# Cross-attention in tile pairs: context projections one tile less ahead of the scores, no extra projection where the pairs begin, and GpSimd takes a tile's keys before the next context

## The reference

```
x = x + cross_attention(layernorm(x), context)   # context: 6272 x 256, 32 heads of 8, RMS norm of q and k
x = x + self_attention(layernorm(x))             # 64 tokens, 16 heads of 128, weights = codes * scales
x = x + experts(layernorm(x))                    # 8 experts (top 2) and a shared one
```

## Time and profile before

| what | value |
|---|---|
| median of the runs | 207.59 us |
| profiled execution: device time, span | 208.22 us, 206.4 us |
| TensorE matmul busy | 193.7 us (94%) |
| ScalarE busy | 148.6 us (72%) |
| VectorE busy | 124.7 us (60%) |
| GpSimd busy | 109.5 us (53%) |
| granted TensorE clock | full in all 40 slices |
| DMA engines, mean busy share | 90% or more in nearly every slice of the cross-attention |

### The profile page before, as it was taken

How to read it: one execution, slowest core, us unless ns; L and a number is a source line. 1 busy time by engine, 2 the same in 40 slices (tenths; PEclk the granted TensorE clock), 3 DMA queues, 4 the chain that set the end, 5 groups by cost and what they waited for, 6 DMA issues and landing times.

```text
span 206.4 us, 7072 instructions
## 1 busy us (share of the span) xinstructions
PE 193.7 (94%) x2625; PEld 133.0 (64%) x2625; DVE 124.7 (60%) x326; ACT 148.6 (72%) x286; POOL 109.5 (53%) x131
## 2 busy tenths in 40 slices
PE   7796987999999999999999999999997989999995
PEld 3364564777777777777777777777764553559554
DVE  1588868566767766677676667767533052463680
ACT  2474885889888888998888889888869912342240
POOL 6445759488666848857684885768475001000100
PEclk9999999999999999999999999999999999999999
DMA  6679999999999999999899899999985599100000
GB/s 195 174 195 205 169 234 213 211 175 245 248 208 237 215 223 233 173 259 210 216 210 240 215 210 254 207 259 203 254 198 110 174 405 430 64 0 3 3 0 13
DMA packets 66549, 39.70 MB, mean 192 GB/s; under 512 B 53858, under 2 KB 60642, under 8 KB 66402
## 3 DMA queue, kind: packets, MB, share of 16 engines
q1 hardware_dynamic: 66098, 38.98, 85.8%
q10 hardware_dynamic: 432, 0.46, 0.7%
HBM read 26.52 MB, written 0.07 MB: 129 GB/s over the span
## 4 chain that ended last, share of the span: by engine, by line
PE 71%; ACT 7%; issue 6%; DMA 5%; DVE 5%; POOL 3%; SPq 1%; DVEq 0%; ACTq 0%; POOLq 0%
PE ps L885 17%; PE ps L907 10%; PE ps L862 10%; PE ps L910 8%; PE ps L913 8%; PE ps L960 5%; ACT room L464 4%; DMA kT<-k 3%; PE ps L1054 3%; DMA wkv_f<-xwkv 2%; PE ps L1013 2%; PE ps L1072 2%; PE ps L819 1%; POOL w_all L385 1%; PE ps L999 1%
## 5 line engine op out<-in xcount | busy, mean ns | idle before, releaser
L464 ACT ACTIVATE room<-ps 128x1024 f32<-128x1024 f32 x98 | 95.3, 1023 | 1.8 <-PE ps L862 1.6
L403 POOL TENSOR_TENSOR ctx_lo<-ctx_f,ctx_hi 128x256 fp32r<-128x256 f32 x49 | 36.0, 734 | 43.6 <-DVE ctx_hi L640 40.6
L885 PE MATMUL ps<-room,v_sb 128*27 128x192 f32 (+1 forms) x1176 | 48.4, 310 | 0.2 <-ACT room L464 0.2
L907 PE MATMUL ps<-wkv_hi,ctx_hi 128*128 128x512 f32 x98 | 41.9, 428 | 2.4 <-DVE k L671 2.1
L910 PE MATMUL ps<-wkv_lo,ctx_hi 128*128 128x512 f32 x98 | 39.0, 398 | 1.2 <-DVE wkv_lo L592 1.2
L885 PEld LDWEIGHTS ps<-room,v_sb 128*27 128x27 f32 (+1 forms) x1176 | 32.8, 103 | 11.0 <-ACT room L464 0.6
L385 POOL TENSOR_TENSOR w_all<-w_all,s_ring 128x1024 f32<-128x1024 f32 x16 | 38.2, 2390 | 0.0
L647 DVE TENSOR_REDUCE k_ss<-k_sq 128x32 f32<-128x256 f32 x49 | 20.3, 415 | 29.2 <-ACT k_sq L471 29.2
L390 POOL TENSOR_TENSOR k<-k_n,k 128x256 f16<-128x256 f32 x49 | 32.9, 673 | 6.7 <-DVE k L671 6.7
L862 PE MATMUL ps<-q_blk,kT 48*128 48x128 f16 x784 | 31.5, 218 | 3.9 <-ACT room L464 2.1
L862 PEld LDWEIGHTS ps<-q_blk,kT 48*128 48x128 f16 x784 | 22.0, 94 | 19.1 <-issue 11.0
(11 more groups left out here) (117 smaller groups left out, 134.2 us busy)
## 6 DMA issues: line engine op xcount, KB each, us to landing
w_all<-codes SPq DMA_DIRECT2D x16, 512.0 KB, 4.2
ctx_f<-ctx_t SPq DMA_DIRECT2D x48, 128.0 KB, 3.6
up_sb<-up_w SPq DMA_DIRECT2D x5, 704.0 KB, 7.4
s_ring<-scales SPq DMA_DIRECT2D x12, 256.0 KB
s_ring<-wo_scales SPq DMA_DIRECT2D x4, 512.0 KB
dn_sb<-down_w SPq DMA_DIRECT2D x1, 1792.0 KB, 14.0
kT<-k SPq DMA_TRANSPOSE x49, 4.3
wkv_f<-xwkv SPq DMA_DIRECT2D x1, 256.0 KB, 3.9
```

The costliest lines, as they stand in the source:

```text
L403: nc.gpsimd.tensor_tensor(ctx_lo[:, split.slot(2)], ctx_f[:, split.slot(4)], ctx_hi[:, split.slot(2)].bitcast(F32), ALU.subtract).then_inc ...
L464: nc.scalar.activation(probs[:, t.probs_slot(), half], ps_scores[half].rearrange("p b n -> p (b n)"), ACT.Exp).then_inc(exp_done, 1)
L885: last = nc.tensor.matmul(ps_o[bank][CT * j:CT * j + heads * VW, at:at + heads * N], v_sb[:, t.slot(8), slot:slot + heads].rearrange("p h ...
L907: nc.tensor.matmul(dst, ctx_hi[:, a, c], wkv_hi[:, c], start=(c == 0), stop=False)
```

## The change

The distances become PROJ = 5, KV = 4, TR = 3, and the pairs now run from step 5 to step 44 = T-5. An odd step t of the pairs is scores(t), projections of t+4 and t+5; the even step is as before. So the first tile that is projected in a pair is now odd, where it was even. In the steps by themselves at the beginning, step 3 now makes scores(3), values(2) and projection 8, step 4 scores(4) and values(3) and no projection, and step 5 starts the pairs with projections 9 and 10. At the end step 43 makes projections 47 and 48 one behind the other (before, step 43 was by itself, with values(42) and projection 48), and step 44 makes values(42) and values(43). ScalarE's special case for step 3 goes. On GpSimd the second part of the keys of tile t+3 now always stands ahead of `ctx_lo` of tile t+6; the multiplications of the weights stay behind the same pair of tiles. The two runs of zero matmuls behind the cross-attention become 5 and 2 instead of 7 and 4. VectorE's and SyncE's lists name the same tiles in the same order as before. The hardware loop now begins at step 6 and has 4 rounds as before.

```diff
-PROJ, KV, TR, PV = 5, 5, 4, -1
-FIRST, LAST = -(PROJ + 2), T - PV
-HEAD = 4
-LOOP0 = 4
-PAIR0, PAIR1 = 3, T - PROJ - 2
-ITERS = (T - PROJ - 2 - LOOP0) // U
+PROJ, KV, TR, PV = 5, 4, 3, -1
+FIRST, LAST = -(PROJ + 1), T - PV
+HEAD = KV
+PAIR0, PAIR1 = 5, T - PROJ
+LOOP0 = PAIR0 + 1
+ITERS = (T - PROJ - 1 - LOOP0) // U
...
     (GpSimd)
-                split, keys = t.ahead(PROJ + 2), t.ahead(TR)
-                if keys.exists() and c < -1:
+                split, keys = t.ahead(PROJ + 1), t.ahead(TR)
+                if keys.exists():
                     second_part(keys)
                 if split.exists():
...
-                if keys.exists() and c >= -1:
-                    second_part(keys)
-                u, piece = divmod(c + 1 - DEQ0, DEQ)
+                u, piece = divmod(c - DEQ0, DEQ)
...
     (ScalarE)
-                if t.i is None and t.c == PAIR0:
-                    exps(t, 0)
-                    keys_squared(r.ahead(-1))
-                    exps(t, 1)
-                    keys_rms(r.ahead(-1))
-                else:
-                    exps(t, 0)
-                    exps(t, 1)
+                exps(t, 0)
+                exps(t, 1)
...
     (TensorE)
-                    if kv.exists() and t.c != -1:
+                    if kv.exists() and t.c not in (-1, PAIR0 - 1):
                         project_context(kv)
                 elif t.odd():
+                    project_context(kv.ahead(-1))
                     project_context(kv)
-                    project_context(kv.ahead(1))
                 else:
-                    for k in (pv.ahead(-1), pv):
-                        for group in range(len(GROUPS)):
-                            values(k, group)
+                    all_values(pv.ahead(-1))
+                    all_values(pv)
...
-            keep_busy(7)
+            keep_busy(5)
...
-            keep_busy(4)
+            keep_busy(2)
```

More of the change, by code:

```diff
@@ L97, in probs_slot, with singly @@
         return 0 if self.odd() else 1 + self.c // 2 % 2
+    def singly(self):
+        return self.i is None and not PAIR0 <= self.c <= PAIR1
     def count(self, per=1, plus=0):
@@ L490, in step @@
                 r = t.ahead(KV)
-                if singly(t):
-                    r = t.ahead(KV - 1 if t.c < PAIR0 else KV)
+                if t.singly():
                     if t.exists():
@@ L628, in split_context @@
             def split_context(t):
-                split = t.ahead(PROJ + 2)
+                split = t.ahead(PROJ + 1)
                 if split.i is None and split.c < 2:
@@ L691, in step @@
                     keys_scaled(r)
-            steps(dve, step, {-5: queries_squared, -4: queries_placed})
+            steps(dve, step, {-4: queries_squared, -3: queries_placed})
             dve.wait_ge(ready("o_first"), 1)
@@ L914, in project_context, with all_values @@
                 last.then_inc(kv_mm, 1)
+            def all_values(pv):
+                for group in range(len(GROUPS)):
+                    if pv.exists():
+                        values(pv, group)
             def step(t):
-                kv, pv = t.ahead(PROJ), t.ahead(PV)
+                pv, kv = t.ahead(PV), t.ahead(PROJ)
                 for half in range(2):
@@ L920, in step @@
                         scores(t, half)
-                if singly(t):
-                    for group in range(len(GROUPS)):
-                        if pv.exists():
-                            values(pv, group)
+                if t.singly():
+                    all_values(pv)
                     if t.c == 0:
                         project_context(kv.ahead(-1))
-                    if kv.exists() and t.c != -1:
+                    if kv.exists() and t.c not in (-1, PAIR0 - 1):
                         project_context(kv)
                 elif t.odd():
+                    project_context(kv.ahead(-1))
                     project_context(kv)
-                    project_context(kv.ahead(1))
                 else:
-                    for k in (pv.ahead(-1), pv):
-                        for group in range(len(GROUPS)):
-                            values(k, group)
+                    all_values(pv.ahead(-1))
+                    all_values(pv)
             steps(pe, step, {-5: queries_mm, -2: queries_turned})
```

2 lines of the change are left out of this document (removed).

## The result

The changed kernel takes 206.62 us, the median of five executions (205.55 to 210.05), beside 207.79 for the kernel before in the same comparison: a ratio of 0.9924, with an interval of 0.9898 to 0.9951. That is 1.2 to 1.6 us faster, where 3.0 were forecast (204.6), and the time lies 0.12 above the range of 203.5 to 206.5. Two later comparisons gave 206.35 (0.9923, 0.988 to 0.9965) and 207.03 (0.9939, 0.9907 to 0.9972).

What follows compares the result with a forecast made beforehand. TensorE was taken as the bound of the pairs, with ScalarE almost a second. Profiled 208.22 less 2.5 (cross-attention) and 0.45 (zero matmuls) gave 205.3, less 0.63 to the median 204.6 us; range 203.5 to 206.5.

Steps and rivals of the forecast that it cites:

- What bounds the kernel: Pairs of tiles: TensorE is the bound with a beat of 5.98 us, ScalarE almost a second bound.
- Opening: Steps 3 to 7: projections 8 and 9 stop waiting, tile 7's exponentials at 40.9 instead of 43.38, 2.5 us earlier.
- The first rival: Opening half won: new waits or late keys 5 leave a gain of 1.2 instead of 2.5; 206.3 us, chance 0.20.
- GpSimd's order: Keys ahead of ctx_lo on GpSimd: turnings issue sooner; ctx_lo 0.67 later within a cover of 1.0, so costs nothing.
- the reorder does nothing: Rival: turning waits behind a load anyway, six first tiles miss by 0.8; 208.7's size, within that rival's chance of 0.09.
- Keys' slack: Keys' time before their scores falls to 9.7 and 11.9 us; waits at tiles 40, 41, 43, 0.8 in sum.
- End: From tile 43's exponentials to the last values: ScalarE's 1.79 wait gone, 14.3 us against 14.7.
- Zero matmuls: Behind the cross-attention and ahead of the third norm: shorter runs of zeros save 0.25 and 0.2, together 0.45 us.
- The rule on the clock: Fewer zeros in a wait could drop TensorE's clock to half behind them; as a rival 208 us, chance 0.02.
- Keys as the bound of the middle: Rival: with transfers of 5.4, six first tiles behind a multiplication wait 0.75 each; 208.7 us, chance 0.09.
- no keys late at all: Fourth rival: no scores wait for keys, so the 0.8 us drops out; 203.8 us, chance 0.14.
- Sum: Whole kernel: profiled execution 208.22 less 2.5 and 0.45 is 205.3; median 0.63 below that, 204.6 us.

Runs made afterwards that it cites:

- e1: Changed kernel with only the shift of the pairs: GpSimd's old order and zero matmuls of 7 and 4 kept; 215.36 us, ratio 1.0365.
- e3: Kernel before with only the zero matmuls changed, 5 and 2 instead of 7 and 4; 207.36 us, ratio 0.9984.
- e7: Kernel before with only the end changed: steps 43 and 44 a pair, tile 48's logarithm and exponential between tile 44's halves; 205.86 us, ratio 0.9912.
- e2: Kernel before with only GpSimd's order changed, the keys' second part always ahead of ctx_lo; 207.49 us, ratio 0.9996.
- a2: The changed kernel measured a second time, nothing altered; 206.35 us over nine executions, ratio 0.9923.
- a10: The changed kernel measured a third time, nothing altered; 207.03 us over 12 executions, ratio 0.9939.
- e6: Kernel before with its old key lead kept, pairs from step 5, another end, GpSimd's new order, zeros 5 and 2; 204.75 us, ratio 0.987.
- e8: Changed kernel with tile 48's logarithm and exponential between the halves of tile 44's exponentials; 205.74 us, ratio 0.9909.
- e9: Changed kernel with SyncE's loads of scales issued one tile later; 206.33 us, ratio 0.9919.
- e11: The same kernel as e6, measured once more beside the changed kernel; 204.54 us, ratio 0.9825.
- e4_light: Changed kernel loading only 16 columns of each piece of codes and scales, multiplications on a cleared buffer (two memsets); 205.08 us, ratio 0.9878.
- e5_light: Changed kernel loading only 16 columns of each piece, without the two memsets, multiplications reading other resident data; 204.59 us, ratio 0.9838.

## Why the prediction was wrong

The mechanisms came as forecast: both gaps closed, and keys became late. The step that failed is the term for late keys, 0.8 us in the sum. The profiles show 1.5, 2.75 and 2.5 in its place (1.8 by the medians), and 1.15 and 1.25 of it in the two typical executions lie in the end, which the sum had at nothing: above all the landing of tile 48, which had been priced at 0.6 and then left out. The second step that failed is the subtraction of 0.63 from a profiled execution to the median.

- **What bounds the kernel: right.** Steady beats of 5.98 us (107.55 / 18 = 5.975 with no key late).
- **Opening: right.** Forecast 12.26 from scores(3) to tile 7's exponentials, 12.12 without late keys, 12.17 to 12.51 with them. "So its wait is gone" held for both projections. The first rival named tile 5's keys, and they did come late, but it put the opening's gain at 1.2, and it is 2.2 to 2.6 (14.74 less 12.12 to 12.51). That its sum, 206.3, lies near the measured time is luck.
- **GpSimd's order: right for its other side** (no wait of TensorE for `ctx_lo` in the pairs), **and undervalued.** The rival "the reorder does nothing" put its absence at 208.7; without it the kernel took 213.0 to 217.5. Six tiles times 0.8 was the wrong form of sum, since tiles of the opening and of the end were late as well: these make 6.6 of the 8.84 us of waits.
- **Keys' slack: the step that failed.** "I take 0.8 for the sum" stood beside tiles 40, 41 and 43. The three profiles give C less 107.55: 1.07, 1.25 and 1.16. To that come 0.39, 0.35 and 0.05 in the opening and 0.06, 1.15 and 1.25 in D. Tiles 40 and 41 were expected and were late in every profile of the changed kernel. Two things in the working were off.

  First, "5.0 at most before 118 us" was the longest of one execution of one kernel. Four profiles with GpSimd's old order (before, e1, e3, e7) have 5.0 to 5.9 there; eight with its new order and the full loads (e2, after, a2, a10, e6, e8, e9, e11) have 6.2 to 7.3, and between 28 and 60 us a median of 4.8 to 5.3 against 4.3 to 4.8. So the longer transfers go with the earlier turnings of the new order, though barely where the opening is the old one (e2: 6.2 and 4.8); what makes them longer is not shown.

  Second, "the turning is issued 0.05 behind" leaves out SyncE's own time. In the kernel before this was there already: tile 8's turning begins 1.48 after its second part. In order of time on the changed kernel's queue around tile 5 (turning 4, context 11, scales, turning 5), then around tile 14 (turning 13, context 20, scales, turning 14):

```profile
25.28 1.23 SPq L309 DMA_TRANSPOSE kT<-k  x1
26.61 0.72 SPq L301 DMA_DIRECT2D ctx_f<-ctx_t  x1
27.39 0.66 SPq L318 DMA_DIRECT2D s_ring<-scales  x1
28.14 1.84 SPq L309 DMA_TRANSPOSE kT<-k  x1
```
```profile
54.10 1.24 SPq L309 DMA_TRANSPOSE kT<-k  x1
55.45 0.51 SPq L301 DMA_DIRECT2D ctx_f<-ctx_t  x1
56.02 0.66 SPq L318 DMA_DIRECT2D s_ring<-scales  x1
56.77 1.26 SPq L309 DMA_TRANSPOSE kT<-k  x1
```

  Tile 14's second part ended at 55.41; its turning begins at 56.77, 1.36 later, because issuing takes the queue 2.67 us from one turning to the next there. Tiles 5 and 8 lose 1.42 and 1.31 in the same place of the order, and both come late in all three profiles (transfers of 6.0 to 6.8 on top). The prediction watched the first tiles of pairs (13, 19, 25, 31), which were never late in the changed kernel.
- **End: the mechanism right (14.31), the typical size not.** "What is late next is this landing: at 4.1 instead of 3.1 it costs 0.6" was priced and left out of the sum. It was 4.45 and 4.55 in the two typical executions, tile 46 was late before it, and D 15.46 and 15.56: 1.2 to 1.3 over the forecast. This is the largest missing term of these two.
- **Zero matmuls: right**, 0.45. The rule on the clock that was weighed against it did nothing here: the granted clock is 1.00 in the stretch behind the shortened run (166.00 to 168.00) and in every later slice:

```profile
166.00:168.00 2.00, 1.61 (x10) 0.94 (x10) 1.67 (x10) 0.20 (x1) 0.00 (x0) 1.00 1.07 418
```

- **The other rivals.** Keys as the bound of the middle (208.7) did not come about with GpSimd's new order; no keys late at all (203.8) is what e4_light and e5_light had to be built for.
- **Sum: the subtraction failed.** "The median of the runs was 0.63 below the profiled one" was carried over from one kernel to the other. For the changed kernel the median lies 1.07 above its profiled execution. The forecast for that execution, 205.3, missed by 0.25; with 0.63 and 1.07 this is 1.95 of the 2.0 missed. That the 0.25 is so small is the luck of a fast execution; the two typical ones (206.35 and 206.90) miss by 1.1 and 1.6. Put the other way, by e5_light: late keys cost 1.8 instead of 0.8, and 204.59 without any stands 0.8 above the 203.8 of the fourth rival, about the 0.63 that did not carry over.

Before, the keys had 13.3 and 14.3 us and only tiles 40 and 41 were near their limit, so the time hardly depended on the transfers. With 9.7 and 11.9 the set of late tiles differs from execution to execution (tile 11 in two of the three profiles, 17 and 23 in one, 48 in two). That this also makes the spread of the times is argued and not shown: part A moves by up to 2.7 us as well.

What stays open: why GpSimd's new order goes with longer transfers in the opening, and why even the kernel without weight traffic has executions in two groups (203.5 to 204.1 and 205.1 to 205.6); of these only one was profiled.

## What to carry to other kernels

Slack before a DMA is insurance: when an edit spends it, take the wait from the longest transfer of several executions plus the issuing queue's own time per DMA, for every position in the period, and put it into the sum. One profile is one draw; when the slack is gone, do not carry a median minus a profiled time from the old kernel to the new one (-0.63 became +1.07 here). An edit that is worth nothing by itself (the order on one engine) can be what makes another possible, so it must be tested with it. And a kernel that wins the ends without spending the lead in the middle was here the better one.

## What the runs showed of the hardware

Two VectorE instructions took as long as the GpSimd memsets beside them. In e4_light, VectorE's and then GpSimd's order of time near the start:

```profile
3.61 1.98 DVE L552 TENSOR_SCALAR spread<-twins,row_sum 128x128 f32<-128x128 f32 x1 [0.68 <-POOL twins L368]
3.81 1.78 DVE L555 BATCH_NORM_STATS2 bn<-x_sb 128x6 f32<-128x128 f32 x1
```
```profile
3.44 0.28 POOL L371 CAST ident<-ident 128x128 f16<-128x128 f32 x1
3.68 1.83 POOL L373 MEMSET s_ring<- 128x1024 f32 x2
```

Without the memsets (e5_light, and the changed kernel) the same two VectorE instructions take 0.29 us each. With them both end at 5.59, 0.08 behind the memsets' end (5.51). The Trainium skill, page "SBUF — State Buffer", section "Who interferes with whom", says that VectorE in its two-port mode and GpSimd share a pair of ports that one instruction holds for its whole time, and that `tensor_scalar` can enter that mode. The trace fits this for the first instruction (1.98 instead of 0.29 us); it does not show the mode, nor that the second instruction only stood behind the first.

The granted clock falls early in some executions, not by the change: e2_pool, which has the opening of the kernel before, falls to 0.57 at 20 us. In the changed kernel's profile:

```profile
14.00:16.00 2.00, 1.24 (x12) 0.59 (x10) 1.97 (x6) 0.10 (x1) 0.18 (x2) 1.00 1.23 210
16.00:18.00 2.00, 1.34 (x18) 1.08 (x19) 1.68 (x6) 1.04 (x4) 1.23 (x2) 0.81 0.92 269
18.00:20.00 2.00, 2.00 (x6) 1.52 (x5) 1.68 (x5) 1.10 (x4) 1.38 (x3) 0.50 1.16 174
```

At 0.50, the lower level of 1.2 GHz, a matmul of 512 columns takes 0.63 us instead of 0.40. Ahead of it TensorE was busy for 1.24 and 1.34 of 2 us. The kernel before was busy for only 0.78 between 16 and 18 us in its profile and kept 1.00. But a2_after, the changed kernel again, was busy for 1.18 and 1.32 us in the same two stretches and kept 1.00 as well, so this busy time does not decide it. Executions with a mean of 0.992 and of 1.00 are found in both kernels.
